# Turned maxima before the modulation rows on the sync engine, and six idle products before the first score

## What is computed

```
mod = silu(c) @ w_adaln + b_adaln
sh_msa, sc_msa, g_msa, sh_mlp, sc_mlp, g_mlp = split(mod, 6)
h = layernorm(x) * (1 + sc_msa) + sh_msa
q, k, v = (h @ w_qkv + b_qkv) by heads
attn = softmax(q @ k.T * hd ** -0.5)
x = x + g_msa * ((attn @ v) @ w_proj + b_proj)
xn = layernorm(x) * (1 + sc_mlp) + sh_mlp
x = x + g_mlp * mlp(xn)          # layer 0: one MLP; layer 1: top 2 of 4 experts
```

## Time and profile before

| | us |
|---|---|
| median of 3 runs | 1539.19 |
| lowest and highest | 1531.56, 1539.38 |
| the profiled execution's own time | 1537.64 |
| its span, first to last instruction | 1535.9 |
| TensorE, VectorE, ScalarE, GpSimd busy | 1398.4, 1094.9, 837.1, 631.3 |

### The profile page before, as it was taken

How to read it: one execution, slowest core, us unless ns; L and a number is a source line. 1 busy time by engine, 2 the same in 40 slices (tenths; PEclk the granted TensorE clock), 3 DMA queues, 4 the chain that set the end, 5 groups by cost and what they waited for, 6 DMA issues and landing times. The chain is left out here.

```text
span 1535.9 us, 27833 instructions
## 1 busy us (share of the span) xinstructions
PE 1398.4 (91%) x9997; PEld 869.7 (57%) x9997; DVE 1094.9 (71%) x1847; ACT 837.1 (55%) x1575; POOL 631.3 (41%) x870
## 2 busy tenths in 40 slices
PE   5978999999998989989889999999994699999994
PEld 3754333333333778967633333333353699999994
DVE  3546899989992646766579999999647365666653
ACT  3635777877886431155477787787831233333331
POOL 2146533553000435534489887796016112121121
PEclk8986999999999999999689999999997799999997
DMA  7577534543001188427732321130059477676763
GB/s 187 163 175 119 131 89 100 137 107 72 3 3 33 51 244 267 162 70 232 173 57 50 49 49 32 23 47 3 3 199 326 139 231 201 209 232 186 237 198 77
DMA packets 93839, 194.66 MB, mean 127 GB/s; under 512 B 35734, under 2 KB 63448, under 8 KB 90716
## 3 DMA queue, kind: packets, MB, share of 16 engines
q1 hardware_dynamic: 61802, 117.93, 24.3%
q0 software_dynamic: 31600, 73.00, 21.2%
q10 hardware_dynamic: 306, 2.00, 0.6%
HBM read 127.27 MB, written 66.68 MB: 126 GB/s over the span
## 5 line engine op out<-in xcount | busy, mean ns | idle before, releaser
L1120 ACT ACTIVATE att_probs<-att_scores 128x512 f32<-128x512 f32 x1002 | 541.6, 604 | 141.0 <-PE att_scores L1271 132.7
L1135 DVE TENSOR_REDUCE att_neg_max<-att_for_max 128x1 f32<-128x1024 f32 x472 | 569.8, 1222 | 49.7 <-PE att_for_max L1228 40.5
L1283 PE MATMUL att_out<-att_probs,V 128*32 128x256 f32 (+1 forms) x3232 | 308.8, 454 | 2.9 <-ACT att_OZ L1097 1.9
L1228 PE MATMUL att_for_max<-att_KS,att_QS 54*128 54x512 f32 x640 | 243.7, 455 | 6.7 <-DVE att_neg_max L1135 6.7
L1271 PE MATMUL att_scores<-att_QS,att_KS 56*128 56x512 f32 x618 | 226.9, 453 | 0.9 <-DMA att_QS<-att_neg_max_rows 0.9
L2177 ACT ACTIVATE experts_gelu<-experts_proj,experts_b 128x256 f32<-128x256 f32 x171 | 81.1, 474 | 208.4 <-PE experts_proj L2246 187.8
L2246 PE MATMUL experts_proj<-experts_x_parts,w_parts 128*128 128x256 f32 (+1 forms) x1197 | 174.0, 286 | 1.2 <-DVE experts_x_parts L1984 1.2
L1271 PEld LDWEIGHTS att_scores<-att_QS,att_KS 56*128 56x128 f32 x618 | 95.0, 185 | 132.5 <-ACT att_probs L1120 116.6
L2135 POOL DMA_INDIRECT sums_of_experts<-experts_y,experts_rows x38 | 61.1, 1608 | 260.1 <-DVE experts_y L2020 254.3
L2246 PEld LDWEIGHTS experts_proj<-experts_x_parts,w_parts 128*128 128x128 f32 (+1 forms) x1197 | 157.8, 191 | 5.2 <-issue 3.6
L1271 PE MATMUL att_scores<-QS,KS 56*128 56x512 f32 x384 | 147.9, 463 | 12.9 <-DMA QS<-att_neg_max_rows 10.3
(11 more groups left out here) (297 smaller groups left out, 2204.4 us busy)
## 6 DMA issues: line engine op xcount, KB each, us to landing
w_parts<-w_parts SPq DMA_DIRECT2D x19, 2304.0 KB
qk_halves<-qkv_qk_parts SPq DMA_DIRECT2D x40, 288.0 KB
w_parts<-w_parts SPq DMA_DIRECT2D x4, 2592.0 KB
slot_rows<-mlp_blank_rows SPq DMA_DIRECT2D x2, 5145.0 KB
att_QS<-qk_halves POOLq DMA_DIRECT2D x120, 72.0 KB, 4.5
att_KS<-qk_halves POOLq DMA_DIRECT2D x60, 144.0 KB, 4.9
w_parts<-w_parts SPq DMA_DIRECT2D x19, 432.0 KB
experts_rows<-slot_rows SPq DMA_DIRECT2D x19, 294.0 KB, 9.8
```

What stands on the lines that cost most here:

```text
L1120: nc.scalar.activation(PR[st % 2][:, j, :], score_bank(st, n), ACT.Exp, scale=SCALE).then_inc(exp_done, 1)
L1135: nc.vector.tensor_reduce(negm[half][:, c:c + 1], psM[ring % 2][:].rearrange("p a n -> p (a n)"), AX_X, ALU.max, negate=True).then_inc(rin ...
L1228: last = nc.tensor.matmul(psM[ring % 2][:, keys, :], QS[s][rows, half, p, t * P:(t + 1) * P], KS[s][rows, p, keys * BLK:(keys + 1) * BLK], ...
L1283: last = nc.tensor.matmul(psO[32 * j:32 * j + 32, n0:n1], T.V[:, g, k, 32 * j:32 * j + 32], PR[st % 2][:, j, n0:n1], start=(k == 0 and n0 ...
```

## The change

In the sync engine's program `store_max(0)` now stands ahead of the loop over `spread_rows`. In TensorE's program `keep_busy` makes six products into `psS[1]`, behind the last head unit (and, in layer 0, the wait for `cols_out`) and ahead of the wait for VectorE's last maximum and the first score. The second edit is in both layers, the first has an effect in layer 0 alone.

```diff
@@ block.sync
                 sp.dma_start(T.ada_scr, arow[:, 0:6 * C]).then_inc(row_stored, 16)
                 sp.wait_ge(row_stored, 16)
+            store_max(0)
+            if early:
                 for dst, part in spread_rows:
                     src = T.ada_scr[:, part * C:(part + 1) * C].rearrange("(o b) c -> o b c", o=1)
                     sp.dma_start(dst, src.broadcast_to([P, B, C])).then_inc(wide_in, 16)
-            store_max(0)
             for j in range(HG):
@@ block.tensor
             if early:
                 pe.wait_ge(cols_out, 1)
+            keep_busy(nc, T, psS[1][:], 6)
             pe.wait_ge(ring_read, HEAD_ITEMS)
             for st in range(STEPS):
```

## The result

Over 20 runs each the changed kernel takes 1528.93 us (median; 1523.59 to 1535.99) and the one before 1537.36 (1529.77 to 1550.07). The ratio is 0.9959, 95% interval 0.9941 to 0.9977: 6.3 us faster, 3.5 to 9.1. The two medians lie 8.4 us apart, a quotient of 0.9945; what follows goes by the ratio. In the profiled execution the span is 1525.6 us, its own time 1527.34. The forecast had the direction and the class (faster, by less than 0.5%), but a sum of 2.4 us. So the question is where the rest came from, and whether the 2.4 are in it at all.

What follows compares the result with a forecast made beforehand. TensorE was taken to be latency-bound at attention start, waiting 6.4 us for maxima loads. Layer 0 -2.4, layer 1 0, idle products 0 to +0.3, set off by faster first scores: 1535.5 us, 8-in-10 range 1530 to 1540.

Steps and rivals of the forecast that it cites:

- a sum of 2.4 us: Whole kernel: layer 0's first score 2.4 us earlier, layer 1 nothing, idle products' cost set off by faster first scores.
- the tail after the last issue goes from 5.09 us to about layer 1's 2.86, a gain of 2.2: Layer 0, last maxima issue to first score: spreads issued later no longer delay the maxima's landing; 2.2 us gained.
- I cost this at nothing: GpSimd behind the third group's loads: early by 2 or late by up to 4 us, hidden before its next deadline.
- near 135: Layer 0, sync engine: issues of the projection-weight loads, moved behind the spreads, start at about 128.8 and end near 135 us.
- rival D: Span 1 start: spreads hold GpSimd back, its transfers meet the maxima later; up to 2.9 us go, 1532.6 us, chance 0.16.
- Both lie in a wait and cost nothing to 0.3 us: Before the first score, both layers: the six idle products fit inside TensorE's wait and cost 0 to 0.3 us.
- That the clock would not pay: First score to first weighing: exponentials set the pace at either clock, so nothing was taken for a higher clock.
- the term that the sum was made of: Layer 0's first score: maxima land earlier, so it starts at 129.7 instead of 132.10, 2.4 us.
- Rival B: Both layers' scores and weighings: idle products raise the clock and it stays up; 4.3 us, 1531.2 us, chance 0.12.
- C: Layer 0's first score: no gain, the 5.09 us come from elsewhere or idle products hold it; 1537.9 us, chance 0.16.
- E: Span 1's first score: moved traffic meets its maxima and it waits longer; +5.6 us, 1543.2 us, chance 0.10.

Runs made afterwards that it cites:

- experiment 2: The kernel before with the six idle products added, order of loads unchanged: ratio to before 1.0045, median 1540.73 us.
- experiment 5: The changed kernel without idle products, with layer 0's 17 projection-weight loads moved ahead of the maxima loads: ratio to before 1.0018, 1535.44 us.
- experiment 10: The kernel before with one wait: in layer 0 GpSimd starts its first weight piece only when span 1's maxima have landed: ratio 0.9946, 1529.72 us.
- experiment 6: The kernel before with one wait: layer 0's projection-weight loads are issued only when the first maxima have landed: ratio 0.9990, 1530.53 us.
- the order alone: The changed kernel without its idle products, measured twice: ratio to before 0.9969 (1530.17 us) and 0.9993 (1531.04 us).
- experiment 12: The changed kernel with the six idle products in layer 1 only: ratio to before 0.9960, 1532.61 us.
- experiment 4: The changed kernel itself, unchanged, measured again: ratio to before 0.9989, 1532.72 us.
- experiment 3: The changed kernel with twelve idle products in place of six: ratio to before 0.9998, 1535.13 us.
- experiment 7: The changed kernel without idle products, GpSimd's 576 KB load moved behind the third group's loads in both layers: ratio to before 1.0001, 1532.90 us.
- experiment 1: The changed kernel without the idle products: ratio to before 0.9969, median 1530.17 us.
- experiment 8: The changed kernel without the idle products, measured a second time: ratio to before 0.9993, 1531.04 us.
- experiment 11: The changed kernel without idle products, layer 1's router load moved late, GpSimd's first piece held for span 1's maxima: ratio to before 0.9983, 1534.18 us.

## Why the prediction was right, and where not

**What bounds the start of a span.** Right as a mechanism: small maxima loads land late because other transfers are in flight. The Trainium skill, "DMA: Bandwidth & Descriptors", section "Queues, rings and completion order", also has a rule that I had not weighed: the increment of a semaphore is ordered behind every earlier write of that DMA engine, across its queues. I read it so that the queue matters less than the backlog. Experiments 2, 5 and 10 agree with that reading: maxima on the sync engine's queue wait 4.37 and 4.69 us behind transfers of GpSimd's queue, and none when those start later. They can't tell this rule from transfers that merely share the DMA engines.

**The step that failed: "the tail after the last issue goes from 5.09 us to about layer 1's 2.86, a gain of 2.2".** The tail did fall, even to 1.42. But it is 1.42 to 1.45 in experiments 2, 6 and 10 too, which have the spreads ahead of the maxima. Of four profiled executions in the old order only the one that I had before me shows 5.09. The spreads were the reason there, as forecast: the last of them landed at 131.2, 4.2 us behind the end of the last maxima issue (127.01). In experiment 2 it landed 0.5 us behind that end (131.1 against 130.67), in 10 at the same moment (128.5, 128.48) and in 6 ahead of it (125.7, 125.92). The head before took 25.77 us from first to last product, those of 2, 10 and 6 took 29.21, 29.11 and 28.40, long enough for the spreads to land. In its first 8 us the head before was granted 1.00, that of 6 0.64, the others 0.50 to 0.51. And the gain at that place, where it was there, isn't what the time shows: experiment 5 has the early first score and is not faster than before, and in the changed kernel's profile the first score comes 32.61 us behind the head's first product, against 31.25. Layer 1's 2.86 was no floor either: those maxima waited for GpSimd's burst, whose last load landed at 769.41. I took a race between the sync engine's and GpSimd's transfers and TensorE's head for a fixed term.

**The second step that failed: "I cost this at nothing"**, of the moved spreads and GpSimd. The delay was found in the right place but from the spreads alone; GpSimd's last wait is for the projection weights behind them, whose issues I let end "near 135" without asking when they land, and which landed near 150. I asked only whether the delay hurts. It is the gain: rival D, to which I gave 0.16 and up to 2.9 us. Experiment 10 does this alone and gains as much (0.9946), experiment 5 takes it away and is slower than the order alone. In the profiles its size is the one that rival D gives: the stretch at span 1 falls from 14.43 us to 11.79 with both edits and to 11.33 in experiment 10, that is by 2.6 and 3.1. Where the transfers meet the maxima squarely (2, 5) the wait is 4.4 to 4.7 us, the low clock follows it, and the stretch takes 17.8 to 19.0; whether executions of the kernel before do that too, no profile shows.

**The idle products.** "Both lie in a wait and cost nothing to 0.3 us" holds in layer 1 (experiment 12). In layer 0 the wait that should cover them ends with VectorE at 1.83 us behind the last product once the maxima land early, and they make it 3.41: +1.58. That the clock would not pay was right, and for the reason given: in the changed kernel it rises in the stretch where the exponentials set the pace (0.80), falls, and the first weighing runs at 1.93 us; in experiments 2 and 4 it didn't rise in layer 0 until the first weighing was over (at 143.1 and 141.7). Alone they make the kernel slower by 0.45%; in the profile it is the stretch at span 1, where TensorE now meets GpSimd's transfers (18.95 us against 14.43).

**The numbers.** -2.4 was forecast and -6.3 (3.5 to 9.1) measured; the median of 1528.93 us lies 1.1 us below the range's lower end of 1530, while the ratio times the 1539.19 that the forecast started from is 1532.9. The other groups give less: 0.9989 for the same kernel. That class and direction came out right is in part luck: the term that the sum was made of gives nothing in the profiled pair, and a gain of like size came from the place that was costed at nothing. Rival B was ruled out by the fall of the clock ahead of the first weighing, and by 3, where it stayed up in layer 0 and the kernel was no faster; C was ruled out by the landing at 129.80, and E never began, since TensorE waited 0.38 us for the maxima of span 1.

**Open.** How often the first maxima land late in the old order: one of four profiles does. Where the rest of the 6.3 us lies: of the profiled pair's difference (1535.9 against 1525.6 us) 2.6 lie at span 1. Another 2.5 lie in layer 0's attention where the clock of the kernel before stood at the low level from 332.1 to 338.9 and the changed one's didn't; experiments 5 and 7 have the same drop, 1 to 4 don't, and nothing ties it to the edits. The time from the last weighing of layer 0 to the head of layer 1 goes from 251.7 to 259.7 us over the 14 profiles, more than the whole effect. Also why experiments 6 and 8 show only 0.1% with a stretch as short as that of 1, and why the combination in 11 isn't as fast as 10; their intervals overlap.

## What to carry to other kernels

When a load on the critical path is small, look for what else is in flight at its issue on all queues, and look at more than one execution before a tail of a few microseconds is taken as fixed. Before a shorter gap is counted as a gain, look whether the work in front of it took as long. Holding a bulk transfer back until the small load has landed cost one wait instruction here and gave as much as the whole change. An idle product is free only as long as the wait that covers it is there, and the first edit took that wait away.

## What the runs showed of the hardware

A set of four 4 KB loads landed 1.41 to 1.45 us after the end of its last issue in layer 0 of the changed kernel and of all twelve experiments, where what had been issued before it had landed, or did so within half a microsecond. In traffic the same loads landed 5.23 us after it in layer 0 of the kernel before and up to 5.41 us in layer 1 (experiment 8). In layer 1 they landed 0.9 to 1.5 us behind the last load of GpSimd's burst in 12 of the 14 profiles, although their own last issue had ended up to 5.4 us earlier; in experiments 7 and 11 the burst was through first, and they landed 1.42 and 1.92 us after their own last issue. In the changed kernel the burst begins with the row at 739.62 and the score starts 18.4 us later; before, the same load began at 752.36 and the score at 770.73, also 18.4.

```profile
739.62 0.59 POOL L1067 DMA_DIRECT2D att_w_gate_rows<-in_L_cond_w_gate_dram  x1 [0.30 <-POOL att_KS L998]
...
749.84 3.26 SPq L950 DMA_DIRECT2D QS<-att_neg_max_rows  x4
...
752.58 0.62 PE L1310 MATMUL att_for_max<-KS,QS 54*128 54x512 f32 x1
...
757.99 0.76 PE L1272 MATMUL att_scores<-QS,KS 56*128 56x512 f32 x1 [1.92 <-DMA QS<-att_neg_max_rows]
```

In the heads of 21 to 29 us TensorE was busy nearly all the time with products of 54 rows. Once its clock had fallen there to the low level (granted 0.50 to 0.51), it stayed at that level through the rest of the head. Behind twelve idle products of 128 rows it came up ahead of the first weighing in both layers (experiment 3, at 133.1 and 761.1 us). Behind six it did so in two of seven places: layer 0 of the changed kernel (133.0) and layer 1 of experiment 2 (771.2), and not in layer 0 of experiments 2 and 4 or layer 1 of the changed kernel, 4 and 12.
